# A third PSUM bank for the maximum pass, and softmax sums inverted by way of three small transfers

## The reference

```python
x = x + tanh(g_xattn[0]) * attention(layernorm(x), ctx, ctx)   # 16 batches, 8 heads, head depth 16
x = x + tanh(g_ffn[0]) * moe(layernorm(x), wg, W, b)           # top-1 of 8 experts, softmax gate
# attention: sm = softmax(einsum('bdm,bdn->bmn', qh, kh) / sqrt(16), axis=-1)
#            ret = einsum('bmn,bcn->bcm', sm, vh)
# moe: idx = argmax(softmax(x @ wg)); out = gate * (W[idx] @ x + b[idx])
```

## Time and profile before

| | us |
|---|---|
| median of three runs | 586.19 |
| the profiled execution, as timed | 586.99 |
| its span in the trace | 585.4 |
| TensorE busy / VectorE busy | 524.5 / 442.1 |
| ScalarE busy / GpSimd busy | 349.5 / 369.9 |

### The profile page before, as it was taken

One profiled execution on the slowest core, in us unless ns is written; L12 is line 12 of the kernel. 1 busy time (PEld: TensorE's weight loads), 2 busy tenths in 40 slices (PEclk: granted clock), 3 DMA queues, 4 the chain that ended last, 5 costly groups with the idle time before them and its releaser, 6 DMA issues.

```text
span 585.4 us, 9717 instructions
## 1 busy us (share of the span) xinstructions
PE 524.5 (90%) x2603; PEld 178.2 (30%) x2603; DVE 442.1 (76%) x868; ACT 349.5 (60%) x429; POOL 369.9 (63%) x630
## 2 busy tenths in 40 slices
PE   0489999899999999999989999999998989899993
PEld 0012223232323232322323232323232235345451
DVE  5897898888898988989898989898998575112121
ACT  3227686868687777778676868776666842111110
POOL 7455577857675866767666787786555446544531
PEclk9999999999999999999999999999999989999997
DMA  4865547775757476554627354535331054633410
GB/s 141 236 151 184 171 151 205 231 201 163 198 160 234 133 210 179 190 181 128 198 63 215 113 167 108 165 98 139 93 108 40 25 181 165 194 129 101 137 40 0
DMA packets 39077, 86.74 MB, mean 148 GB/s; under 512 B 12498, under 2 KB 14546, under 8 KB 39008
## 3 DMA queue, kind: packets, MB, share of 16 engines
q1 hardware_dynamic: 26944, 61.17, 36.4%
q0 software_dynamic: 12096, 25.13, 13.5%
HBM read 63.24 MB, written 28.18 MB: 156 GB/s over the span
## 4 chain that ended last, share of the span: by engine, by line
PE 45%; DVE 36%; issue 7%; POOL 4%; ACT 4%; DMA 3%; POOLq 0%; DVEq 0%; ACTq 0%; SPq 0%
DVE neg_max L862 23%; PE ps_pv L1243 13%; PE ps_ring L1202 11%; PE ps_scores L1302 10%; PE ps_scores L1224 6%; ACT probs L779 3%; DVE neg_max L1075 3%; PE ps_pv L1252 2%; DVE den_turned L888 1%; PE ps_scores L1283 1%; DMA stacks<-shift_parts 1%; PE ps_pv L1260 1%; DVE st L904 1%; PE ps_ring L1210 1%; DVE st L873 1%
## 5 line engine op out<-in xcount | busy, mean ns | idle before, releaser
L862 DVE TENSOR_REDUCE neg_max<-ps_ring 128x1 f32<-128x512 f32 x480 | 312.3, 681 | 42.5 <-PE ps_ring L1202 41.7
L779 ACT ACTIVATE probs<-ps_scores 128x1024 f32<-128x1024 f32 x256 | 250.0, 1021 | 72.0 <-PE ps_scores L1224 69.4
L1202 PE MATMUL ps_ring<-stacks 96*128 96x512 bf16 x480 | 180.2, 388 | 16.0 <-DVE neg_max L862 5.8
L1224 PE MATMUL ps_scores<-stacks 128*128 128x512 bf16 x512 | 153.9, 383 | 4.7 <-ACT probs L779 2.8
L1243 PE MATMUL ps_pv<-probs,v_ones 128*32 128x512 f32 x1024 | 137.9, 611 | 0.3 <-DVE logits L914 0.3
L1202 PEld LDWEIGHTS ps_ring<-stacks 96*128 96x128 bf16 x480 | 46.1, 96 | 191.5 <-DVE neg_max L862 173.1
L1302 PE MATMUL ps_scores<-w_sb,f_xt 128*128 x184 | 83.2, 593 | 0.0
L1224 PEld LDWEIGHTS ps_scores<-stacks 128*128 128x128 bf16 x512 | 48.1, 101 | 49.6 <-ACT probs L779 16.1
L556 POOL DMA_DIRECT2D stacks<-shift_parts x96 | 49.4, 518 | 20.6 <-POOL shift_parts L547 17.6
L772 ACT COPY f_xt<-ps_scores 128x512 f32<-128x512 f32 x23 | 13.5, 586 | 71.9 <-PE ps_scores L1283 71.9
L1302 PEld LDWEIGHTS ps_scores<-w_sb,f_xt 128*128 128x128 f32 x184 | 34.4, 190 | 33.0 <-issue 32.2
(11 more groups left out here) (144 smaller groups left out, 509.2 us busy)
## 6 DMA issues: line engine op xcount, KB each, us to landing
stacks<-parts_dram SPq DMA_DIRECT2D x224, 64.0 KB, 2.6
parts_dram<-prep POOLq DMA_DIRECT2D x15, 768.0 KB
w_sb<-w_t SPq DMA_DIRECT2D x16, 512.0 KB, 6.1
recs_dram<-rec SPq DMA_DIRECT2D x16, 512.0 KB, 4.3
stacks<-parts_dram SPq DMA_DIRECT2D x32, 192.0 KB, 3.1
prep<-x_perm SPq DMA_DIRECT2D x16, 256.0 KB, 3.1
prep<-k_perm SPq DMA_DIRECT2D x16, 256.0 KB, 3.4
v_in<-v_t SPq DMA_DIRECT2D x16, 256.0 KB, 3.5
```

The lines of the kernel that those rows point to most:

```text
L779: nc.scalar.activation(probs[:, k % 2, 2 * jp:2 * jp + 2], ps_scores[:, jp], ACT.Exp).then_inc(exp_done, 1)
L862: nc.vector.tensor_reduce(neg_max[:, g, j, c:c + 1], ps_ring[:, u.slot(n)], AX.X, ALU.max, negate=True).then_inc(ring_free, 1)
L1202: nc.tensor.matmul(ps_ring[:, u.slot(n + c)], q_stack[0:KS, B.p, g, j, c * 128:(c + 1) * 128], k_stack[0:KS, B.p, g, j], start=True, stop= ...
L1224: last = nc.tensor.matmul(ps_scores[:, jp, j % 2], k_stack[0:KA, B.p, g, j, c * 128:(c + 1) * 128], q_stack[0:KA, B.p, g, j], start=True, ...
```

## The change

PSUM is dealt out anew. ps_ring grows from two to three banks, ps_pv shrinks from two to one, so low and high values share a bank; with 4 for ps_scores it is 8 banks either way. The rows of `turn_rows` and the logits and ranks, which stood in ps_pv, now take a turn in the ring. A table ENTRIES gives each entry its slot, and `holder` finds whom a matmul waits for.

The sums of batches 0 to 13 no longer pass VectorE's transposes. ScalarE's copies keep the rows of sums (the gates get a 1 there); SyncE copies these rows into a tile of 128x16 (`take_sums`); VectorE inverts it (`invert_taken`); SyncE stores it in DRAM (`store_recips`) and reads it back four times, each to 16 partitions (`spread_recips`). GpSimd then multiplies each half apart (`add_low`, `add_high`), four products and sums where there were three. Batches 14 and 15 keep the old way.

In the diff the first piece is the allocation, then come SyncE's functions and their place in batch B (behind the store of batch B-2's record), VectorE's inversion and its order, ScalarE's order after the exponentials of step k, and VectorE's constants at the start.

```diff
-        ps_ring = ctx.enter_context(nc.psum_tensor("ps_ring", [128, 2, DM], F32))
-        ps_pv = ctx.enter_context(nc.psum_tensor("ps_pv", [128, NG, DM], F32))
+        ps_ring = ctx.enter_context(nc.psum_tensor("ps_ring", [128, 3, DM], F32))
+        ps_pv = ctx.enter_context(nc.psum_tensor("ps_pv", [128, DM], F32))
...
+            def take_sums(B, g):
+                sp.wait_ge((low_read, high_read)[g], B.b + 1)
...
+                of = (low_num[DH:128:32], high_num[0:128:32])[g]
+                sp.dma_start(sums[:, g], of.rearrange("j (t c) -> j t c", c=DM // 32)).then_inc(sums_in[g], 16)
+            def store_recips(B, g):
+                wait(sp, recips_in[g], B.b * (16 * NJ))
...
+                sp.wait_ge(sums_inverted[g], B.b + 1)
...
+                sp.dma_start(recip_dram[g].rearrange("j (t c) -> (j t) c", c=DM // 32), sums[:, g]).then_inc(recips_out[g], 16)
+            def spread_recips(B, g):
+                wait(sp, (low_added, x1_done)[g], B.b)
...
+                sp.wait_ge(recips_out[g], B.b * 16 + 16)
...
+                for j in range(NJ):
+                    at = 32 * j + g * DH
+                    sp.dma_start(scale[at:at + DH, g], recip_dram[g, j].partition_broadcast(DH)).then_inc(recips_in[g], 16)
...
+                if prev and by_transfer(B.plus(-1)):
+                    take_sums(B.plus(-1), 1)
+                    store_recips(B.plus(-1), 1)
+                    spread_recips(B.plus(-1), 1)
                 load_residual(B)
...
+            def invert_taken(B, g):
+                dve.wait_ge(sums_in[g], B.b * 16 + 16)
+                nc.vector.reciprocal(sums[:, g], sums[:, g]).then_inc(sums_inverted[g], 1)
...
-                            if at == (0, 3):
-                                turn_sums(attended, 1)
-                            if at == (1, 0):
-                                invert_sums(attended, 1)
-                            if at == (2, 1):
-                                turn_back(attended)
-                            if at == (3, 2):
+                            if at == (3, 1):
+                                invert_taken(attended, 1)
+                            if at == (5, 2):
                                 stats2(attended)
...
-                    if k == (5 if end else 4) and prev:
+                    if k == (5 if end else 6) and prev:
                         norm2(B.plus(-1))
...
+                      lambda: nc.vector.tensor_tensor(low_gate[:], low_gate[:], high_half[:], ALU.add),
+                      lambda: nc.vector.tensor_tensor(high_gate[:], high_gate[:], low_half[:], ALU.add),
+                      lambda: nc.vector.memset(scale[:].rearrange("p g m -> p (g m)"), 0.0)]
```

More of the change, by code:

```diff
@@ L63, with holder @@
 DVE_BATCH, POOL_BATCH = 2, 15
+TURNED = 14
+RANK_AT = 64
+ROWS_SLOT, ROUTE_SLOT = 2, 1
+ENTRIES = (("t00", 1), ("turn1", 0), ("t01", 1), ("t02", 2), ("t03", 0), ("route", 1),
[3 rows of a table added]
+           ("t70", 2), ("t71", 0), ("t72", 1), ("rows", ROWS_SLOT), ("t73", 0))
+SLOT = dict(ENTRIES)
+NUMBER = {name: n for n, name in enumerate(e for e, _ in ENTRIES if e not in ("rows", "route"))}
+def holder(name, route, rows, rows_in_last):
+    names = [e for e, _ in ENTRIES]
+    here = names[:names.index(name)]
+    for e in reversed(here):
+        if SLOT[e] == SLOT[name] and (e != "route" or route) and (e != "rows" or rows):
+            return e, 0
+    for e in reversed(names):
+        if SLOT[e] == SLOT[name] and e != "route" and (e != "rows" or rows_in_last):
+            return e, RING_BATCH
 def phase_of(s):
@@ L108, in stand_alone, with ring_base, by_transfer @@
     eng.nop(nofuse=True)
[L111 to L132, removed]
+def ring_base(B):
+    return B.b * RING_BATCH + RING_FIRST
+def by_transfer(B):
+    return not isinstance(B.b, int) or B.b < TURNED
 def build(nc, x_rows, x_perm, k_perm, v_t, w_t, wg_t, bias, g_attn, g_ffn, out):
@@ L340, in load_residual @@
             def load_residual(B):
-                wait(sp, x1_done, B.b)
+                wait(sp, low_added if not B.known(NB - 1) else x1_done, B.b)
                 if not isinstance(B.b, int):
@@ L755, in read_low, with read_high @@
                 act.wait_ge(pv_done, B.b * STEPS + NC)
+                wait(act, low_added if not B.known(NB - 1) else x1_done, B.b)
+                nc.scalar.mul(low_num[:], ps_pv[:], (low_gate if by_transfer(B) else low_only)[:]).then_inc(low_read, 1)
+            def read_high(B):
+                act.wait_ge(pv_done, B.b * STEPS + STEPS)
                 wait(act, x1_done, B.b)
[L757 to L762, removed]
+                nc.scalar.mul(high_num[:], ps_pv[:], (high_gate if by_transfer(B) else high_only)[:]).then_inc(high_read, 1)
             def exp_gates(group):
@@ L801, in emit @@
                         exp_gates(2)
[L802 removed]
+                    if k == 0 and prev:
                         read_high(B.plus(-1))
@@ L1194, in _, with take_slot, scores_for_max, turn_maxima @@
         def _(pe):
[L1195 removed]
+            def take_slot(B, name, prev, prev2):
+                held, ago = holder(name, prev2, prev, prev2)
+                if held == "rows":
+                    pe.wait_ge(rows_taken, B.b - 1)
+                elif held == "route":
+                    pe.wait_ge(logits_taken, B.b - 1)
+                    for group in range(2):
+                        if B.known(RANKED[group]):
+                            pe.wait_ge(ranks_taken, group + 1)
+                else:
+                    wait(pe, ring_free, ring_base(B) + (NUMBER[held] + 1 - ago))
+            def scores_for_max(B, prev, prev2, k, chunks):
                 g, j = divmod(k, NJ)
+                into = B.plus(1)
                 if j == 0 and 0 in chunks:
[L1199 removed]
+                    pe.wait_ge(stack_in[into.p][g], into.i * (16 * STACK_LOADS) + 16 * STACK_LOADS)
                 for c in chunks:
[L1201 to L1210 removed]
+                    tile = f"t{k}{c}"
+                    take_slot(B, tile, prev, prev2)
+                    nc.tensor.matmul(ps_ring[:, SLOT[tile]], q_stack[0:KS, into.p, g, j, c * 128:(c + 1) * 128],
+                                     k_stack[0:KS, into.p, g, j], start=True, stop=True).then_inc(ring_full, 1)
+            def turn_maxima(g, slot):
+                nc.tensor.transpose(ps_ring[0:NJ * NC, slot, 0:128], neg_max[:, g].rearrange("p j c -> p (j c)"),
                                     identity[:]).then_inc(ring_full, 1)
@@ L1258, in route @@
                 pe.wait_ge(rows_taken, B.b + 1)
+                if isinstance(B.b, int) and B.b > RANKED[1] - 2:
+                    pe.wait_ge(logits_taken, B.b)
                 for c in range(NC):
-                    last = nc.tensor.matmul(rows_bank[:, 0:NE], xt[:, c], wg_sb[:, c], start=c == 0, stop=c == NC - 1)
+                    last = nc.tensor.matmul(route_bank[:, 0:NE], xt[:, c], wg_sb[:, c], start=c == 0, stop=c == NC - 1)
                 last.then_inc(logits_full, 1)
@@ L1267, in rank @@
                 pe.wait_ge(onehot_ready, group + 1)
+                wait(pe, ranks_taken, group)
                 for b in range(n):
```

242 lines of the change are left out of this document (137 added, 105 removed), and 3 rows, old and new, of the table ENTRIES.

## The result

| | kernel before | changed kernel |
|---|---|---|
| time, median (lowest to highest) | 585.6 us (584.2 to 586.4) | 634.1 us (631.8 to 635.9) |
| ratio, 95% interval | 1 | 1.082 [1.080, 1.085] |
| span of the profiled execution, granted TensorE clock | 585.4 us, 0.991 | 634.3 us, 0.961 |
| turned copy at the start of batch 0 | 43.4 us | 45.7 us |
| the 15 intervals from there to the start of batch 15 | 410.4 us | 452.3 us |

What follows compares the result with a forecast made beforehand. The kernel was taken as bound to and fro between VectorE and TensorE. Fourteen loops of 27.0 against 26.94 us add 1, the start 1.8: 587.0 + 2.8 = 589.8, less about 1 for batch 0: 588 us, range 563 to 604.

Steps and rivals of the forecast that it cites:

- The loop: High sums of batch B-1 followed through batch B across engines and DMA, closing once a batch in 27.0 us against 26.94.
- The eight steps: Pieces of the loop from T to the next such maximum, T': 11.0 + 0.3 + 3.8 + 1.3 + 2.6 + 3.8 + 1.4 + 0.9 + 1.9.
- T: Start of the loop, called VectorE's first maximum of batch B; 259.87 in the kernel before.
- 2 to 5, to x1_done: Hand-overs 0.3, two landings 3.8, issuing four reads 1.3, GpSimd's add_high 2.6; x1_done at T + 19.0.
- 6 and 7, to the end of norm 2: GpSimd's split and load of maxima 3.8, rstd2 1.4, then norm2 with a hand-over 0.9; rows normalised at T + 25.1.
- Step 1: VectorE from T to the end of the inversion: T + 12.46 less three pieces gives T + 10.8, with reciprocal 11.0.
- the third rival: Loaded queue: take_sums goes out late behind 1.5 to 2 MB, lands T + 9 to 11; 608 us (596 to 612), chance 0.20.
- two landings: Store of the reciprocals to DRAM and last of four reads back: 1.9 us each, 3.8 together, range 3.2 to 5.2.
- Step 8: ScalarE's exponentials of step 7, next batch's first scores and ring matmul before VectorE starts T': 1.9 us with hand-overs.
- hidden by its idle time: GpSimd's fourth product (1.27 us) less its two spreads was taken to cost nothing, GpSimd being busy 283 of 410.
- The start: VectorE sets five more constants before the first maxima, which wait for them: about 1.8 us.
- The free run: Rival 1: the loop does not bind, a batch falls to 24.8 to 26; 559 up to 570 us, chance 0.17.

Runs made afterwards that it cites:

- e_late: e_win with one operation moved back: VectorE inverts the high sums at step (3, 1) instead of (1, 3); 612.2 us.
- e_early: Changed kernel with the high sums fetched right after the query stacks and inverted after maximum (1, 3) instead of (3, 1); 615.0 us.
- e_best: e_early plus weights and record behind the hand-over, start constants on GpSimd, table fill in batch 9, batch 14's token stores behind the high half; 590.3 us.
- e_win: e_best with table fill in batch 8, bias split in batch 13, batch 14's stores after rstd2, last batch's sums turned first; 577.5 us.
- e_bank: Changed kernel's three ring banks and one values bank, but sums by transposes and spreads as in the kernel before; 592.1 us.
- e_two: e_early plus weights and record behind the hand-over, maxima in two alternating banks, only routing scores and norm 2 rows in the third; 603.6 us.
- e_record: e_early with only the record's store moved behind the hand-over, the weights left ahead; 600.3 us.

## Why the prediction was wrong, step by step

The loop was the right mechanism, and its first step was sized wrong. The eight steps against two traces, in us:

| steps | predicted | changed kernel, T = 251.68 | e_late, T = 207.76 |
|---|---|---|---|
| 1, to the end of the inversion | 11.0 | 14.90 | 13.14 |
| 2 to 5, to x1_done | 8.0 | 7.55 | 7.84 |
| 6 and 7, to the end of norm 2 | 6.1 | 6.05 | 6.04 |
| 8, to T' | 1.9 | 1.03 | 1.12 |
| sum | 27.0 | 29.53 | 28.14 |

- **Step 1 failed, by two causes.** The queue: with it clear in e_late the inversion starts at T + 12.90 and does not wait; in the changed kernel it starts at T + 14.65, having waited 2.01 us. That is the third rival, whose mechanism and mark were right; it had 0.20. It let the sums out at T + 6.5 and in at T + 9 to 11, where they went out at T + 8.5 and were waited for until T + 14.65, and its 29.4 "at worst" was the ordinary batch. The other was in none of the cases: the step takes the three removed pieces off T + 12.46 in full and puts the end of maximum (3, 1) at T + 10.8. What was removed became waiting. From the turned copy to the end of maximum (3, 1) e_late takes 11.1 us (209.56 to 220.66), and the kernel before took 11.2 (261.13 in the earlier trace rows to 272.33). The 1.64 us subtracted were too much to begin with, since VectorE's rows overlap (the 0.70 of the transpose at 269.15 moved its follower by 0.62): outside its waits VectorE needs 1.06 us less. The maxima stand 0.30 + 0.42 + 0.48 + 0.25 + 0.24 = 1.69 us for TensorE in the one and 0.30 + 0.43 = 0.73 in the other, so 0.96 of the 1.06 us went there. Work taken from an engine moves its later instructions forward only as far as it set their time. The other 0.5 is at the turn of the batch, where the two maxima no longer run back to back.
- **Steps 2 to 7 held**: 13.60 and 13.88 us against 14.1, the estimate of 3.8 for two landings with them. The page of the changed kernel gives 1.6 for the 8 KB store and 1.8 for the reads, as medians over the run. What was late there is the transfer ahead of them, for whose landing the page has no number. A median can hide such a case: e_early's page gives 2.2 for the store, whose spread came 6.25 us behind it in a batch with weights.
- **Step 8 was 0.8 too long**: T is the maximum before the batch's own first one, and it needs the turned rows but not the exponentials: in the changed kernel TensorE turns them at 280.33, 0.15 us behind the norm, fills the ring's bank at 280.79, and the maximum starts at 281.21.
- **The sum then fell short.** With 29.5 a batch, 14 x 2.6 = 36 us over the 26.94 of the earlier trace rows; measured 41.9 over all 15 intervals. The rest I read in single batches and tested only in part, by e_best and e_win: where token stores stand on GpSimd, its `rstd1` is late and ScalarE's first norm with it (42.0 us of idle time against 16.4 before). The cost of GpSimd's work was called "hidden by its idle time"; that idle time was itself a wait at the head of an in-order list with some 12 us of work behind it. Last comes what I did not price at all, TensorE's clock (below).
- **The start** cost 2.2 against 1.8, near enough, and with the constants on GpSimd in e_best 0.2 of it is left (43.67 against 43.44). **The free run** exists at 25.6 (24.8 forecast), but only with the inversion at (1, 3) and the queue clear.
- What stays open: why the end costs 4.7 us more. e_bank has 4.0 of it without any transfer and e_win almost none, so I put it down to the single values bank or to the order at the end, which e_win changed in several places at once.

## What to carry to other kernels

When a loop goes over several engines, time each edge by what releases it in the trace: taking work off an engine that is then fed too slowly brings nothing forward. Before a small transfer goes on a loop, list what the same queue issues in the 6 us ahead of it, and put bulk without a deadline behind it; a median landing over the run does not tell. And two halves of a change can be worth nothing apart: e_bank and e_two would each have argued against a change that gives 5% of a batch when its consumers are in time.

## What the hardware showed

A small transfer came late by what stood ahead of it on its queue. The store of 8 KB let the spread go after 1.49 us in the changed kernel (266.67 to 268.16), where no bulk had been issued for the 6.9 us ahead of it; after 2.67 with the record (512 KB) just ahead, 4.95 with the weights (1 MB) and 6.25 with both (e_early, e_record). The Trainium skill, "DMA: Bandwidth & Descriptors", section "Queues, rings and completion order", says that each DMA engine consumes a queue's descriptors in ring order; by that rule a small transfer waits for the data ahead of it. These numbers fit it, though no run here tells waiting in order from sharing the DMA engines with the bulk.

TensorE's clock fell after it had stood. In the changed kernel it did 0.16 us of work between 318 and 320, waiting for VectorE, and the windows that follow read, in the column before the last two, 0.87, 0.50 and 0.78 of the granted clock:

```profile
318.00:320.00 2.00, 0.16 (x1) 0.00 (x0) 1.93 (x5) 2.00 (x4) 1.27 (x1) 1.00 0.25 82
320.00:322.00 2.00, 1.69 (x10) 0.35 (x10) 2.00 (x5) 0.66 (x2) 1.94 (x2) 0.87 0.00 0
322.00:324.00 2.00, 2.00 (x8) 0.58 (x5) 1.12 (x2) 0.01 (x1) 0.34 (x1) 0.50 0.00 0
324.00:326.00 2.00, 2.00 (x13) 0.56 (x11) 1.31 (x3) 1.86 (x2) 0.00 (x0) 0.78 0.00 0
```

0.50 is the lower level, 1.2 of 2.4 GHz. Nine of the 15 intervals of the changed kernel have a mean of 0.94 or 0.95 and one 0.90; before, all had 1.00. A pair of score matmuls took 1.06 us there and 0.60 beside it. The 6.5 us of extra busy time in the first window above bound what this cost directly, and the clock is not what closes the loop at 29.5: the interval from 253.15 has 1.00 and is as long as that from 132.73, which has 0.94 (29.54 and 29.46). So a wait of TensorE can be paid a second time, but the second price was the small one here.
